# Matmuls over 49 and 96 rows in place of 64 and 128 in an attention stage

## The reference

```python
q, k, v = (z.reshape(b, s, H, hd).transpose(0, 2, 1, 3) for z in (q, k, v))   # H = 16, hd = 16, s = 2048
attn = jnp.einsum('bhqd,bhkd->bhqk', q, k) / jnp.sqrt(jnp.float32(d))
attn = jnp.where(causal[None, None], -jnp.inf, attn)
rel_idx = jnp.arange(s)[None, :] - jnp.arange(s)[:, None] + (s - 1)
bias = rpb[rel_idx].transpose(2, 0, 1)      # 1023 rows in the table, indices beyond it are clamped
w = jax.nn.softmax(attn + bias[None], axis=-1)
o = jnp.einsum('bhqk,bhkd->bhqd', w, v)
```

## Time and profile before

| | us |
|---|---|
| median of three runs | 2470.99 (2467.52 to 2474.86) |
| the profiled execution | 2470.99 |
| its span, first to last instruction | 2469.0 |
| PE busy | 2328.9 (94%) |
| DVE busy | 1922.0 (78%) |
| ACT busy | 1425.2 (58%) |
| POOL busy | 1049.3 (42%) |

### The profile page before, as it was taken

The page is one execution under the profiler, slowest core; times in us unless marked ns, Lnnn a source line. Parts: engine busy times, 40 slices in busy tenths (PEclk is TensorE's granted clock), DMA queues, the critical chain, the costliest instruction groups (busy, mean ns, idle before and its releaser), DMA issues. The chain is left out here.

```text
span 2469.0 us, 40630 instructions
## 1 busy us (share of the span) xinstructions
PE 2328.9 (94%) x13523; PEld 1500.3 (61%) x13523; DVE 1922.0 (78%) x4359; ACT 1425.2 (58%) x2608; POOL 1049.3 (42%) x1032
## 2 busy tenths in 40 slices
PE   8999999999999998899999997999999999999992
PEld 5433333333333333577777775888888777887782
DVE  3888888888888881556666656999999989898366
ACT  3477667676667666445454535666565676654420
POOL 3512221111221211100011004999999877898364
PEclk9999999999999999999999998999999999999996
DMA  8643222224322202100000001111111222224794
GB/s 256 176 71 77 52 52 52 52 56 68 82 52 52 52 22 76 61 9 26 19 25 18 9 18 44 52 65 52 65 58 58 71 104 68 73 74 151 225 330 154
DMA packets 111766, 190.04 MB, mean 77 GB/s; under 512 B 15956, under 2 KB 74120, under 8 KB 108360
## 3 DMA queue, kind: packets, MB, share of 16 engines
q1 hardware_dynamic: 84328, 150.22, 23.0%
q10 hardware_dynamic: 21088, 20.45, 2.4%
q0 software_dynamic: 6144, 16.79, 2.1%
HBM read 104.13 MB, written 78.79 MB: 74 GB/s over the span
## 5 line engine op out<-in xcount | busy, mean ns | idle before, releaser
L627 ACT ACTIVATE ssm_in_dt<-att_s 128x512 f32<-128x512 f32 (+3 forms) x1280 | 600.3, 536 | 258.0 <-PE att_s L537 185.0
L537 PE MATMUL att_s<-att_qs,att_ks 64*128 64x512 f32 (+3 forms) x1280 | 444.5, 422 | 27.0 <-ACT ssm_in_dt L627 25.3
L524 PE MATMUL att_s<-att_ks,att_qs 64*128 64x512 f32 (+3 forms) x1280 | 441.9, 424 | 5.9 <-DVE ssm_in_u L761 4.0
L537 PEld LDWEIGHTS att_s<-att_qs,att_ks 64*128 64x128 f32 x1280 | 208.4, 184 | 367.8 <-ACT ssm_in_dt L627 325.1
L1941 PE MATMUL ssm_ps<-ssm_hi,ssm_halves 128*128 128x512 f32 x1024 | 407.1, 398 | 14.2 <-DVE ssm_lo L2399 7.1
L1943 PE MATMUL ssm_ps<-ssm_hi,ssm_halves 128*128 128x512 f32 x1024 | 401.2, 392 | 0.0
L1942 PE MATMUL ssm_ps<-ssm_lo,ssm_halves 128*128 128x512 f32 x1024 | 401.2, 392 | 0.0
L2332 POOL TENSOR_TENSOR ssm_cc<-ssm_cc,ssm_h 128x512 f32<-128x512 f32 x256 | 332.7, 1300 | 74.7 <-DVE ssm_h L2428 64.4
L2341 POOL TENSOR_TENSOR ssm_out_z<-ssm_out_z,ssm_cc 128x512 f32<-128x512 f32 x256 | 339.0, 1324 | 0.1
L448 POOL TENSOR_SCALAR_AFFINE_SELECT ssm_in_dt<-ssm_in_dt 128x256 f32<-128x256 f32 x256 | 104.6, 409 | 543.8 <-ACT ssm_in_dt L627 531.9
L570 PE MATMUL att_o_ps<-ssm_in_dt,att_vst 128*32 128x512 f32 (+3 forms) x2560 | 299.8, 540 | 2.4 <-ACT ssm_in_dt L627 0.8
(11 more groups left out here) (333 smaller groups left out, 3631.8 us busy)
## 6 DMA issues: line engine op xcount, KB each, us to landing
qk_halves<-ssm_in_dt SPq DMA_DIRECT2D x64, 256.0 KB, 3.0
scan_halves<-ssm_halves SPq DMA_DIRECT2D x32, 512.0 KB, 2.9
ssm_halves<-scan_halves SPq DMA_DIRECT2D x32, 512.0 KB, 3.5
moe_sorted<-att_hidden SPq DMA_DIRECT2D x31, 512.0 KB, 9.6
moe_answers<-ssm_cc ACTq DMA_DIRECT2D x62, 256.0 KB, 3.9
att_stage_q<-qk_halves SPq DMA_DIRECT2D x96, 128.0 KB, 4.4
att_stage_k<-qk_halves SPq DMA_DIRECT2D x96, 128.0 KB, 6.0
ssm_raw<-in_w_bc SPq DMA_DIRECT2D x30, 256.0 KB, 3.3
```

What stands on the lines that cost most here:

```text
L524: mm = nc.tensor.matmul(s1[:, S1_BANK[at], 0:hi - lo], qs[p % 3][half(b), I * P:(I + 1) * P], ks[p % 3][half(b), lo:hi], start=True, stop= ...
L537: mm = nc.tensor.matmul(s2[:, turn % RING, 0:hi - lo], ks[p % 3][half(b), J * P:(J + 1) * P], qs[p % 3][half(b), lo:hi], start=True, stop= ...
L627: nc.scalar.activation(prob[:, b, step % 2, x * CH + lo:(x + 1) * CH], s2[:, turn % RING, 0:CH - lo], ACT.Exp, scale=1.0 / HD).then_inc(s2 ...
```

## The change

`score` and `search` contract over 49 rows of each batch's 64 rather than over all 64, and the casts into `ks` and `qs` cover partitions 0 to 112 rather than 0 to 127. The matmuls of `add_far` contract over 96 rows rather than 128: `far` and `flip_b` lose their 32 zero rows, and with them go three fills (two on POOL, one on DVE). Row 64 remains the first row of batch 1.

```diff
+ROWS = 1 + 3 * HD
-        far = [sp.sb(f"far{s}", [P, WIN], BF16) for s in range(2)]
+        far = [sp.sb(f"far{s}", [PARTS * QUARTER, WIN], BF16) for s in range(2)]
-        flip_b = sp.sb("flip_b", [P, QUARTER], BF16)
+        flip_b = sp.sb("flip_b", [PARTS * QUARTER, QUARTER], BF16)
-                step(nc.gpsimd.memset(far[s][PARTS * QUARTER:, :], 0.0))
             def round_stack(p):
-                    nc.gpsimd.tensor_copy(dst[p % 3][:], stage[1 - n][:]).then_inc(stack_ready, 1)
+                    nc.gpsimd.tensor_copy(dst[p % 3][0:P // 2 + ROWS, :], stage[1 - n][0:P // 2 + ROWS, :]).then_inc(stack_ready, 1)
-            eng.wait_ge(pool_set, 13)
+            eng.wait_ge(pool_set, 11)
             def search(p, x, b):
-                mm = nc.tensor.matmul(s1[:, S1_BANK[at], 0:hi - lo], qs[p % 3][half(b), I * P:(I + 1) * P],
-                                      ks[p % 3][half(b), lo:hi], start=True, stop=True)
+                mm = nc.tensor.matmul(s1[:, S1_BANK[at], 0:hi - lo], qs[p % 3][half(b, ROWS), I * P:(I + 1) * P],
+                                      ks[p % 3][half(b, ROWS), lo:hi], start=True, stop=True)
             def score(p, step, x, b):
-                mm = nc.tensor.matmul(s2[:, turn % RING, 0:hi - lo], ks[p % 3][half(b), J * P:(J + 1) * P],
-                                      qs[p % 3][half(b), lo:hi], start=True, stop=not has_far)
+                mm = nc.tensor.matmul(s2[:, turn % RING, 0:hi - lo], ks[p % 3][half(b, ROWS), J * P:(J + 1) * P],
+                                      qs[p % 3][half(b, ROWS), lo:hi], start=True, stop=not has_far)
-            nc.vector.memset(flip_b[PARTS * QUARTER:, :], 0.0)
-            nc.vector.tensor_copy(flip_b[0:PARTS * QUARTER, :], flip[:]).then_inc(const_cast, 1)
+            nc.vector.tensor_copy(flip_b[:], flip[:]).then_inc(const_cast, 1)
-                nc.vector.tensor_copy(dst[0][:], stage[1 - n][:]).then_inc(stack_ready, 1)
+                nc.vector.tensor_copy(dst[0][0:P // 2 + ROWS, :], stage[1 - n][0:P // 2 + ROWS, :]).then_inc(stack_ready, 1)
```

## The result

The changed kernel is slower: 2495.74 us median of 12 runs (2486.45 to 2509.23) against 2469.73 of before in the same session, a ratio of 1.0105 with a 95% interval of 1.0083 to 1.0128. The forecast was 2471 us and no change, its range 2460 to 2480. The profiled execution of after is one of the longer runs, 2505.8 us with a span of 2504.1, 35.1 us above before's 2469.0.

A forecast was written before the change was run, and what follows sets the result against it. The prediction took PE to bound the attention, busy for 846.71 of 880 us. Its terms, 0 + 0 + 0 + 0, left the profiled 2471 us unchanged, with a range of 2460 to 2480.

The forecast's parts named there:

- Instruction prices: Matmuls, weight loads, casts and fills: fewer rows or partitions make none cheaper, and the dropped fills were hidden; 0 us.
- the sum's four zeros: Score and search matmuls, `add_far` matmuls, dropped fills and narrower casts: each 0 us.
- Slower: the clock falls: Rival in the attention: fewer working rows lower PE's clock; +457 us if for all PE work; chance 0.02.
- for a tenth of them +46: Clock rival's smaller price: a tenth of the attention's 846.7 us of PE work at the lower clock, +46 us.
- Pairs fall apart: Rival in score and search: 49-row matmuls no longer run side by side; +152 to +256 us; chance 0.03.
- a few ns each: Rival: each of 2560 score and search matmuls needs 3 ns or more extra; from +7.7 us; chance 0.03.
- gaps shrink: Rival: PE's gaps at changes of matmul shape shrink with the rows; up to -34 us; chance 0.08.
- A clock under 1.00 between 100 and 980 us: Sign in the attention's profile that would show the forecast of no change wrong.

The follow-up runs named there:

- e3_rows33: The changed kernel with 33 rows in place of 49 for score and search, bias matmuls over 96; ratio 1.1494 against before.
- a2_pe_only: The kernel before with only the row counts changed, 49 for score and search, 96 for bias matmuls; fills and casts kept; 2530.72 us, ratio 1.0107.
- d1_zero31: The kernel before, still addressing 64 rows in score and search, but rows 33 to 63 hold zeros and the third part isn't loaded; 2467.45 us, ratio 0.9983.
- a3_33far128: The kernel before with 33 rows in place of 64 for score and search, bias matmuls over 128 rows; ratio 1.1002.
- e4_zeros: The kernel before with zeros in place of ones in the 15 spare rows of `ks`; 2498.55 us, ratio 0.9994.

## Why the prediction was wrong

- **Instruction prices: right.** Loads of 183 ns over 49 rows as over 64, pairs that start together, casts and fills that cost the same or were hidden. Of the sum's four zeros, measured at full clock, each holds to 0.1 us.
- **The step that failed: "Slower: the clock falls", at a chance of 0.02.** The mechanism stood among the rivals, with a price that was nearly right. The ratio 1.54 from the rare slow `L2037` means 1 - 1 / 1.54 = 0.35 us lost for each microsecond at the lower level; the four kernels measured 0.38. Its "for a tenth of them +46" takes a tenth of the work; what came was a tenth of the stage's time, 90 us at 1.2 GHz, priced so at 0.35 x 90 = 32 us and measured at 34.4. What was wrong is the evidence against it. It said that the clock is 1.00 though half the rows stand idle for any single score. But in all heads but the last, scores and searches stand side by side and fill all 128 rows, which the prediction itself had read from the earlier trace rows. Only head 15 has no search, and there before holds 1.00 from 932 to 976 us with 64-row scores and no search beside them (its third line in the section on the result). The prediction didn't name it; it would have been real evidence, and even so it covers 44 us of one head. Nothing in before had fewer rows than 64 and 128 in these instructions, and its clock said nothing on 49 and 96. The second argument, that the clock fell only behind pauses of PE, was true of before and couldn't speak for other row counts.
- **"Pairs fall apart", "a few ns each", "gaps shrink": all refuted.** The pairs start 0.34 us apart and the loads take 183 ns, as said above. The gap rows at changes of shape, over the whole attention, are 64.4 us in 192 and 57.9 us in 222, against 60.0 and 56.7, and the one ahead of L537 58.0 in 114 against 27.7 in 95. They grew; their longest went from 0.4 to 1.7 us (L537), which fits the lower clock.
- **The sign that was named worked.** "A clock under 1.00 between 100 and 980 us" was among the marks that would show the forecast wrong.

The Trainium skill, in "TensorE: Matmul & The Clock Gate", section "What's actually happening", lets the gate follow how busy PE has been, and its table has the lower level after an idle stretch. By that rule the change is worth 0. The trace doesn't agree: PE is busy for 39.95 of 40 us at 0.50 above, and for 99.28 of 100 us in `e3_rows33`. The measurement decides. Of the rule for loads in its section "Step-by-step: what each phase is for", the trace agrees that the number of rows doesn't matter: 183 ns over 49 rows and over 64.

The cause is shown for the row counts in TensorE's instructions (`a2_pe_only` against before, `d1_zero31` against `a3_33far128`). How they count isn't: before's head 15 holds 1.00 with 64-row scores and no search, while after falls in heads with a score and a search of 49 rows each, so the rows of those two alone don't say where it falls. Whether those of the weight loads or of the matmuls count wasn't tried, since one number sets both. Why a given head falls and its neighbour doesn't stays open: the changed kernel's 45 recorded runs span 32 us (2485.23 to 2517.45), and their mean clocks 0.958 to 0.975.

## What to carry to other kernels

Padding rows can cost a matmul no time (15 of 64 here) and yet hold up TensorE's clock; before stripping them, look at the granted clock of the whole stage, and after it look again over several runs. When a change alters how much of the array works without altering any instruction's price, the clock is the first rival, not the last. Two halves that are harmless alone (0.18% and 0.06%) can cost 1% together, so test the whole.

## What the hardware showed unexpectedly

- TensorE at 1.2 GHz with PE busy for 99.28 of 100 us, in one stage of a one-core kernel; the rows that the instructions address decide over it, and the data don't (64 rows addressed, 31 of them zeros: 1.00 from 200 to 300 us).
- The loss grows steeply, not in proportion. Beside 96 bias rows, going from 64 to 57 rows costs 0.3%, the next 8 rows 0.7% more, the next 8 another 2 to 4%, and the last 8, to 33, some 11%.
- The same program took 2470 us in two sessions and 2499 us in two others (before, medians), with a mean clock of 0.981 in the fourth and 0.978 in the second and third. It isn't the chip alone: the second and the fourth are recorded on the same one. Most of it lies far behind the attention: between the first and the last start of the experts' bias matmul (L2037 of before) lie 165.5 us in before's trace and 192.4 in that of `e4_zeros`, from a session of 2499. Why is open.
